# The reciprocal root of 128x64 mean squares: GpSimd pow in place of a bit estimate with Newton steps on VectorE

## The chip, the cores and the metric

The kernel runs on one core of one Trainium2 chip. The metric is the time of one execution on the device, in microseconds (us). The time before is the median of three runs. Beside it stands one profiled execution, whose trace is read below. Engines are named as in the profile: PE is TensorE's matmul, PEld its weight load, DVE VectorE, ACT ScalarE, POOL GpSimd, SP SyncE.

## The reference

One decoder layer works on x of 16 sequences, 128 tokens and 256 features, in float32. It has three parts, each added to its input and followed by a layer norm: an attention without softmax, a causal convolution of products with a context, and a feed-forward part with 4-bit weights. The change is in the attention:

```python
q = (q @ fq1_w.T + fq1_b) * (q @ fq2_w.T + fq2_b)       # k likewise; 16 heads of 16
s = jnp.where(mask, einsum('bhncd,bhnmd->bhncm', qc, kc), 0.0)
o = (inter + intra).reshape(B, H, L, dk)
o = o * jax.lax.rsqrt(jnp.mean(o * o, axis=-1, keepdims=True) + EPS) * norm_w
o = o.transpose(0, 2, 1, 3).reshape(B, L, D)
return o @ wo.T
```

So each token has 16 mean squares, one for each head, and each needs the reciprocal of its root.

## The kernel before

The 16 sequences go in four groups (g = 0 to 3) of NB = 4 sequences, 512 tokens. While the attention and the convolution of group g run (the front), the feed-forward part of group g-1 runs between them on the same engines, in 16 slots; group 0 has no such partner, and the last group's feed-forward part runs alone at the end. `schedule` writes the order out by hand, and every engine runs its own list in this one order, so an engine that waits holds up all that stands behind it in its list. In a slot the parts of the feed-forward are `gate`, `up` and `down`, and after each comes a third of the slot's front stages:

```python
slots[4] = [("sums", 0), ("sums", 1), ("rms", 0)]
slots[5] = [pause, pause, ("wide", 0)]
slots[6] = [("factor", 0), pause, pause]
slots[7] = [("outproj", 0), ("outproj", 1), pause]
slots[8] = [("norm", 0), pause, ("x1T", 0)]
```

The stages around the change are these. `squares` (ACT, L522) squares the attention's output. `sums` (PE, L973) sums the squares of each head with a matmul into 128x64 values in PSUM, 64 being 4 sequences by 16 heads. `rms` (DVE, L686 to L704) makes `mean_sq` of them and from that `inv_rms`. `wide` (ACT, L528) copies each of the 64 values 16 times, to 128x1024. `factor` transposes that on PE (L984), copies it out of PSUM on ACT (L535), and multiplies the attention's output by it on DVE (L710). `outproj` is the output projection (PE, L991), `norm` the first layer norm, whose reciprocal root is two pows of 128x2 values on POOL (`rstd`, L383).

The feed-forward part of a slot is: `gate` and `up` matmuls on PE (`split_mm`, L904 to L906), the gelu on ACT (L579), `inner` on DVE (L855, which waits for `up` and the gelu), `inner_hi` on ACT (L585), `split` on DVE (L849), and the `down` matmuls of the slot before. The 4-bit weights are unpacked beside group 0 and part of group 1, a piece at a time, by `unpack` on DVE (L634, L641, L651, L655) and ACT (L483, which waits for L634). In group 0 a piece follows the stage `rms`; in group 1 a piece opens every slot.

POOL has nothing in the stages `sums`, `rms`, `wide` and `factor` in the kernel before: its last work before them is a spread of q for the scores (L389), and its next is `rstd` of the first layer norm.

Of the kernel before, what the change touches and what calls it, by code (L numbers as in the profile page):

```python
# [14 lines left out]
I32 = mybir.dt.int32  # L15
ALU = mybir.AluOpType
# [3 lines left out]
P = 128  # L20
B, S, D = 16, 128, 256
H, DK = 16, 16
NB = 4
# [12 lines left out]
NIBBLE = (1 << 31) | (7 << 22)  # L36
LN_EPS = 1e-5
RMS_EPS = 1e-5
STEPS = 10


def count(eng, sem, per_group, g, k):

    value = per_group * g + k
    if value <= 0:
        return
    eng.wait_ge(sem, value)
# [6 lines left out]
def decoder_layer(nc, x, xT, ctx, ctxT, wq, wk, wvT, woT, fT, bias, skip, toep,  # L54
# [7 lines left out]
    with ExitStack() as stack:  # L62
        def sb(name, shape, dt=F32):
            return stack.enter_context(nc.sbuf_tensor(name, shape, dt))

        def sem(name):
            return stack.enter_context(nc.semaphore(name))
# [18 lines left out]
        minus_half = sb("minus_half", [P, 1])  # L86
# [23 lines left out]
        ctx_sb = sb("ctx_sb", [P, NB, D])  # L110
        mean_sq = sb("mean_sq", [P, NB * H])
        inv_rms = sb("inv_rms", [P, NB * H])
        newton = sb("newton", [P, NB * H])
        ve = sb("ve", [P, 3, NB])
        st = sb("st", [P, 3, NB, 6])
        mv = sb("mv", [P, 3, NB, 2])
# [19 lines left out]
        def sems(*names):  # L136
            return [sem(n) for n in names]
# [19 lines left out]

        dve_const, bd_ready, qk_ready, sm_ready, on_ready, z_ready, conv_ready = sems(
            "dve_const", "bd_ready", "qk_ready", "sm_ready", "on_ready", "z_ready", "conv_ready")
        ms_ready, newton_step, rms_ready, half_ready, sk_ready, x2lo_ready, inter_ready, ilo_ready = sems(  # L160
            "ms_ready", "newton_step", "rms_ready", "half_ready", "sk_ready", "x2lo_ready", "inter_ready", "ilo_ready")
        nibble_ready, bits_ready, deq_ready, wlo_ready = sems(
            "nibble_ready", "bits_ready", "deq_ready", "wlo_ready")

# [40 lines left out]
        conv = [("conv", h) for h in range(CH)]  # L205
# [15 lines left out]
        def with_piece(name, k):  # L221

            return name in ("rms", "factor", "norm", "x1T") or name == "score" and k % 2 == 1
# [6 lines left out]
        def schedule(eng, turn, front, gate, up, down, unpack, finish):  # L230

            pieces = iter(range(NU + 2))

            def beside(times=1):
                for _ in range(times):
                    for n in pieces:  # L240
                        unpack(n)
                        break

            def run(g, stages):
                for name, k in stages:
                    if name in front:
                        front[name](g, k)

            def slot(prev, g, s, times=(0, 0, 0)):
                each = -(-len(slots[s]) // 3)  # L250
                for i, part in enumerate((gate, up, down)):
                    beside(times[i])
                    part(prev, s)
                    if g is not None:
                        run(g, slots[s][i * each:(i + 1) * each])

            beside(START)
            turn(None, None, 0, lambda pair: beside(pair % 2))
            for s in range(NT):
                for stage in slots[s]:  # L260
                    run(0, [stage])
                    if with_piece(*stage):
                        beside()
            turn(None, 0, 1, lambda pair: beside(pair // 2))
            for s in range(NT):
                slot(0, 1, s, SECOND[s])
            for g in range(2, G):
                turn(g - 2, g - 1, g)
                for s in range(NT):
                    slot(g - 1, g, s)  # L270
            turn(G - 2, G - 1, None)
            for s in range(NT):
                slot(G - 1, None, s)
            finish()
# [80 lines left out]
        def _(pool):  # L355
# [23 lines left out]
            def rstd(g, ln):  # L379

                for j in range(2):
                    count(pool, ve_ready[ln], 2, g, j + 1)
                    nc.gpsimd.tensor_tensor(ve[:, ln, 2 * j:2 * j + 2], ve[:, ln, 2 * j:2 * j + 2],  # L383
                                            minus_half[:].broadcast_to([P, 2]), ALU.pow).then_inc(rstd_ready[ln], 1)

            def spread(g, v):

                mt, b = spread_waits(pool, g, v)
                nc.gpsimd.tensor_tensor(qbd[:, v % 2, :].rearrange("p (h c) -> p h c", c=S),  # L389
                                        qT_sb[:, mt, b * S:(b + 1) * S].unsqueeze(1).broadcast_to([P, 4, S]),  # L390
                                        quad_sel[:].unsqueeze(2).broadcast_to([P, 4, S]),
                                        ALU.mult).then_inc(spread_ready[1], 1)

            def score(g, v):

                if v + 2 < 8 and v % 2:
                    spread(g, v + 2)

            def norm(g, _):
                rstd(g, 0)  # L400

# [33 lines left out]
            def turn(done, prev, g, beside=nothing):  # L435
# [6 lines left out]
                if done is not None:  # L442
# [2 lines left out]
                    count(pool, res_ready, NB, done, NB)  # L445
                    pool.dma_start(out_v[:, bass.ds(at, NB), :], res_sb).then_inc(stored, 16)

            schedule(pool, turn, {"score": score, "norm": norm, "x1T": x1T, "conv": conv}, nothing, nothing, nothing, nothing,
                     lambda: rstd(G - 1, 2))


        @block.scalar
        def _(act):
# [70 lines left out]
            def wide(g, _):  # L524

                count(act, ms_mm, 2, g, 2)
                count(act, rms_ready, 1, g, 1)
                nc.scalar.activation(rms_sb[:].rearrange("p k (n e) -> p (k n) e", e=DK),  # L528
                                     inv_rms[:].unsqueeze(2).broadcast_to([P, NB * H, DK]), ACT.Copy)\
                    .then_inc(wide_ready, 1)  # L530

            def factor(g, _):
                for mt in range(KT):
                    count(act, rT_mm, 2, g, mt + 1)
                    nc.scalar.activation(fac_sb[:, mt, :], fb[mt][:, :], ACT.Copy).then_inc(rT_ready, 1)  # L535

            def x1T(g, _):
                for j in range(KT):
                    count(act, x1T_mm, 2, g, j + 1)
                    nc.scalar.activation(x1T_sb[:, j, :], fb[2 + j][:, :], ACT.Copy).then_inc(x1T_ready, 1)  # L540
# [52 lines left out]
        def _(dve):  # L593
# [88 lines left out]
            def rms(g, _):  # L682
                count(dve, ms_mm, 2, g, 2)
                if g:
                    count(dve, wide_ready, 1, g, 0)
                nc.vector.tensor_scalar(mean_sq[:], fb[0][:, 0:NB * H], 1.0 / DK, RMS_EPS, ALU.mult, ALU.add)\  # L686
                    .then_inc(ms_ready, 1)


                count(dve, ms_ready, 1, g, 1)  # L690
                nc.vector.tensor_scalar(newton[:].bitcast(I32), mean_sq[:].bitcast(I32), 1, None,
                                        ALU.logical_shift_right).then_inc(newton_step, 1)
                count(dve, newton_step, STEPS, g, 1)
                nc.vector.tensor_scalar(inv_rms[:].bitcast(I32), newton[:].bitcast(I32), -1, 0x5f3759df,
                                        ALU.mult, ALU.add).then_inc(newton_step, 1)
                for i in range(3):
                    count(dve, newton_step, STEPS, g, 3 * i + 2)
                    nc.vector.tensor_tensor(newton[:], inv_rms[:], inv_rms[:], ALU.mult).then_inc(newton_step, 1)
                    count(dve, newton_step, STEPS, g, 3 * i + 3)
                    nc.vector.scalar_tensor_tensor(newton[:], newton[:], -0.5, mean_sq[:], ALU.mult, ALU.mult)\  # L700
                        .then_inc(newton_step, 1)
                    count(dve, newton_step, STEPS, g, 3 * i + 4)
                    nc.vector.scalar_tensor_tensor(inv_rms[:], newton[:], 1.5, inv_rms[:], ALU.add, ALU.mult)\
                        .then_inc(rms_ready if i == 2 else newton_step, 1)  # L704

            def factor(g, _):
                count(dve, o_mm, 8, g, 8)
# [149 lines left out]
            def finish():  # L857
# [19 lines left out]
                for b in range(NB):  # L877
                    dve.wait_ge(rstd_ready[2], 2 * g + b // 2 + 1)
                    nc.vector.tensor_scalar(res_sb[:, b, :], res_sb[:, b, :], mv[:, 2, b, 0:1], ve[:, 2, b:b + 1],
                                            ALU.subtract, ALU.mult).then_inc(res_ready, 1)  # L880

            schedule(dve, turn, {"score": score, "rms": rms, "factor": factor, "outproj": outproj, "norm": norm,
                                 "conv": conv}, nothing, inner, split, unpack, finish)

# [274 lines left out]
```

## Time and profile before

| what | value |
|---|---|
| median of 3 runs | 585.72 us (584.79 to 586.55) |
| the profiled execution's own time | 585.73 us |
| span of its instructions | 584.0 us |
| mean granted TensorE clock | 0.963 |
| busy: PE, DVE, ACT, POOL | 532.6, 382.8, 157.0, 133.5 us |

The span runs from the first to the last instruction; 1.7 us of the execution's own time lie around it. Busy time is the sum of an engine's instructions. An engine's idle time costs only where the engine that sets the end waits for it. The granted clock is a share of TensorE's full rate.

### The profile page before, as it was taken

What the parts mean: (1) busy time and instruction counts of PE and PEld (TensorE: products, weight loads), DVE (VectorE), ACT (ScalarE), POOL (GpSimd) and SP (SyncE); (2) the same over time, 40 slices, a digit from 0 to 9 for tenths busy, and PEclk for the clock granted to TensorE, in tenths of its full rate; (3) what the DMA queues carried; (4) which work ended last, traced back from release to release, by engine and by line L of the source; (5) the groups of instructions that cost most, each with busy time, mean ns of one, the idle gap of its engine ahead of it and who ended that gap; (6) DMA issues with size and microseconds to landing.
All of it is one profiled execution on the core that took longest, in us unless ns stands there. A gap on an engine that the chain in (4) does not pass through costs nothing.

```text
span 584.0 us, 8537 instructions
## 1 busy us (share of the span) xinstructions
PE 532.6 (91%) x3152; PEld 426.8 (73%) x3152; DVE 382.8 (66%) x814; ACT 157.0 (27%) x291; POOL 133.5 (23%) x195
## 2 busy tenths in 40 slices
PE   5974699889999899999999999999999999599994
PEld 4733477746878788755888888856888887488883
DVE  4595799877688976875454767865454667633334
ACT  3432101352343112242232111342322111132220
POOL 2020285110004453121004452120014451200001
PEclk9995789989999999999999999999999999699998
DMA  7411332221121110031001110040001110100001
GB/s 204 119 52 42 95 108 70 66 66 33 36 80 51 52 46 9 1 114 68 1 0 46 53 40 10 0 145 1 1 5 54 44 47 0 36 1 2 0 1 36
DMA packets 25258, 26.80 MB, mean 46 GB/s; under 512 B 2817, under 2 KB 22785, under 8 KB 25217
## 3 DMA queue, kind: packets, MB, share of 16 engines
q1 hardware_dynamic: 14208, 15.73, 9.2%
q10 hardware_dynamic: 10576, 8.95, 5.3%
q0 software_dynamic: 432, 1.57, 0.8%
q8 instruction: 25, 0.41, 0.3%
q14 instruction: 17, 0.13, 0.1%
HBM read 24.15 MB, written 2.10 MB: 45 GB/s over the span
## 4 chain that ended last, share of the span: by engine, by line
PE 80%; DVE 12%; issue 3%; ACT 2%; POOL 1%; DMA 1%; ACTq 0%; POOLq 0%; DVEq 0%
PE bank L904 18%; PE bank L906 17%; PE bank L905 17%; PE bank L1014 5%; PE bank L951 5%; PE bank L1015 5%; PE bank L1017 4%; PE bank L991 3%; PE bank L961 2%; DVE qbd L677 2%; DVE weight L634 1%; PE bank L973 1%; DMA wo_sb<-in_woT 1%; PE bank L1023 1%; DVE ffn_lo L641 1%
## 5 line engine op out<-in xcount | busy, mean ns | idle before, releaser
L904 PE MATMUL bank<-x2T_lo,ffn_hi 128*128 128x512 f32 x256 | 111.8, 437 | 5.2 <-DVE x2T_lo L839 4.8
L855 DVE TENSOR_TENSOR inter<-bank,inter 128x512 f32<-128x512 f32 x64 | 44.2, 690 | 100.0 <-PE bank L906 99.8
L906 PE MATMUL bank<-x2T_hi,ffn_hi 128*128 128x512 f32 x256 | 102.5, 400 | 0.0
L905 PE MATMUL bank<-x2T_hi,ffn_lo 128*128 128x512 f32 x256 | 102.4, 400 | 0.0
L433 POOL TENSOR_TENSOR qbd<-qT_sb,ctxT_sb 128x256 f32<-128x256 f32 x128 | 80.4, 650 | 81.7 <-PE bank L1017 66.6
L383 POOL TENSOR_TENSOR ve<-ve,minus_half 128x2 f32<-128x2 f32 x24 | 16.9, 723 | 278.8 <-DVE ve L727 207.9
L904 PE MATMUL bank<-ffn_lo,inter_hi 128*128 128x256 f32 x256 | 77.1, 301 | 1.2 <-DVE inter_lo L849 0.8
L585 ACT ACTIVATE inter_hi<-inter 128x512 fp32r<-128x512 f32 x64 | 40.4, 632 | 138.5 <-DVE inter L855 138.5
L906 PE MATMUL bank<-ffn_hi,inter_hi 128*128 128x256 f32 x256 | 72.0, 281 | 0.0
L905 PE MATMUL bank<-ffn_hi,inter_lo 128*128 128x256 f32 x256 | 71.9, 281 | 0.0
L579 ACT ACTIVATE inter<-bank 128x512 f32<-128x512 f32 x64 | 38.1, 595 | 116.6 <-PE bank L906 116.5
L849 DVE TENSOR_TENSOR inter_lo<-inter,inter_hi 128x512 fp32r<-128x512 f32 x64 | 50.4, 787 | 23.8 <-PE bank L906 16.1
L904 PEld LDWEIGHTS bank<-x2T_lo,ffn_hi 128*128 128x128 f32 x256 | 48.9, 191 | 19.9 <-issue 8.5
L906 PEld LDWEIGHTS bank<-x2T_hi,ffn_hi 128*128 128x128 f32 x256 | 48.9, 191 | 12.0
L905 PEld LDWEIGHTS bank<-x2T_hi,ffn_lo 128*128 128x128 f32 x256 | 49.0, 192 | 8.3
L904 PEld LDWEIGHTS bank<-ffn_lo,inter_hi 128*128 128x128 f32 x256 | 48.2, 188 | 5.0 <-ACT inter_hi L585 2.0
L905 PEld LDWEIGHTS bank<-ffn_hi,inter_lo 128*128 128x128 f32 x256 | 48.4, 189 | 1.8
L764 DVE TENSOR_TENSOR qbd<-bank,ctxT_sb 128x256 f32<-128x256 f32 x128 | 47.7, 413 | 2.4 <-PE bank L1017 2.4
L906 PEld LDWEIGHTS bank<-ffn_hi,inter_hi 128*128 128x128 f32 x256 | 48.1, 188 | 0.0
L769 DVE TENSOR_REDUCE gate_q<-qbd 128x64 f32<-128x512 f32 x64 | 43.9, 686 | 2.2
L1014 PE MATMUL bank<-qbd,toep_sb 128*128 128x256 f32 x128 | 39.9, 394 | 4.1 <-POOL qbd L433 2.6
L951 PE MATMUL bank<-qbd,kT_sb 64*128 64x512 f32 x128 | 36.2, 644 | 3.2 <-DVE qbd L677 2.7
(116 smaller groups left out, 796.5 us busy)
## 6 DMA issues: line engine op xcount, KB each, us to landing
toep_sb<-in_toep ACTq DMA_DIRECT2D x64, 128.0 KB, 2.1
xT_sb<-in_xT SPq DMA_DIRECT2D x4, 512.0 KB, 5.9
ctxT_sb<-in_ctxT SPq DMA_DIRECT2D x4, 512.0 KB, 4.8
x_sb<-in_x SPq DMA_DIRECT2D x4, 512.0 KB, 5.9
ctx_sb<-in_ctx SPq DMA_DIRECT2D x4, 512.0 KB, 6.8
out<-ctxT_sb POOLq DMA_DIRECT2D x3, 512.0 KB, 3.4
raw_w<-in_gate_p SPq DMA_DIRECT2D x8, 128.0 KB, 2.3
raw_s<-in_gate_s SPq DMA_DIRECT2D x8, 128.0 KB
```

Of the source, the lines that this page charges most:

```text
L433: nc.gpsimd.tensor_tensor(pairs(kv_sb, h % 2)[:, kt], v_i, c_j, ALU.mult).then_inc(kv_ready, 1)
L579: nc.scalar.activation(inter[:, n % 2, :], gate_ps[:, :], ACT.Gelu_apprx_tanh).then_inc(gelu_ready, 1)
L585: nc.scalar.activation(inter_hi[:, n % 2, :], inter[:, n % 2, :], ACT.Copy).then_inc(ihi_ready, 1)
L764: last = nc.vector.tensor_tensor(pairs(z_sb, h % 2)[:, lt], fb[h % 2][:, :].rearrange("p (k b j i) -> p k b j i", k=KT, b=NB, i=CI)[:, lt] ...
L769: nc.vector.tensor_reduce(conv_sb[:, :, :, h * CI:(h + 1) * CI], pairs(z_sb, h % 2), AX.X, ALU.add)\
L849: nc.vector.tensor_tensor(inter_lo[:, n % 2, :], inter[:, n % 2, :], inter_hi[:, n % 2, :].bitcast(F32), ALU.subtract).then_inc(ilo_ready, 1)
L855: nc.vector.tensor_tensor(inter[:, n % 2, :], up_ps[:, :], inter[:, n % 2, :], ALU.mult).then_inc(inter_ready, 1)
L904: nc.tensor.matmul(ps, w_hi, x_lo, start=start, stop=False, skip_group_check=True)
L905: nc.tensor.matmul(ps, w_lo, x_hi, start=False, stop=False, skip_group_check=True)
L906: return nc.tensor.matmul(ps, w_hi, x_hi, start=False, stop=stop, skip_group_check=True)
L951: last = nc.tensor.matmul(score_ps(g, v)[r][:, :], kT_sb[rows, mt, b * S:(b + 1) * S], qbd[rows, v % 2, :], start=True, stop=True)
L1014: nc.tensor.matmul(fb[h % 2][:, 0:n], diag, kv[:, 0:n], start=True, stop=True)
```

## The change

The stage `rms` of DVE keeps its first instruction, which makes `mean_sq`. Its eleven others are taken out: a shift, a multiply-add on the bits, and three rounds of three Newton instructions, each of which waits for the one before. In their place POOL gets a stage `rms` with one instruction, a tensor_tensor with pow of the 128x64 `mean_sq` and a constant -0.5 that is broadcast over the 64 columns. `wide` on ACT waits for it as it did for the last Newton instruction. The tile `newton` and its semaphore are gone.

```diff
-        newton = sb("newton", [P, NB * H])
...
+            def rms(g, _):
+
+                count(pool, ms_ready, 1, g, 1)
+                nc.gpsimd.tensor_tensor(inv_rms[:], mean_sq[:], minus_half[:].broadcast_to([P, NB * H]), ALU.pow)\
+                    .then_inc(rms_ready, 1)
+
...
-            schedule(pool, turn, {"score": score, "norm": norm, "x1T": x1T, "conv": conv}, nothing, nothing, nothing, nothing,
+            schedule(pool, turn, {"score": score, "rms": rms, "norm": norm, "x1T": x1T, "conv": conv}, nothing, nothing, nothing, nothing,
...
                 nc.vector.tensor_scalar(mean_sq[:], fb[0][:, 0:NB * H], 1.0 / DK, RMS_EPS, ALU.mult, ALU.add)\
                     .then_inc(ms_ready, 1)
-
-
-                count(dve, ms_ready, 1, g, 1)
-                nc.vector.tensor_scalar(newton[:].bitcast(I32), mean_sq[:].bitcast(I32), 1, None,
-                                        ALU.logical_shift_right).then_inc(newton_step, 1)
-                count(dve, newton_step, STEPS, g, 1)
-                nc.vector.tensor_scalar(inv_rms[:].bitcast(I32), newton[:].bitcast(I32), -1, 0x5f3759df,
-                                        ALU.mult, ALU.add).then_inc(newton_step, 1)
-                for i in range(3):
-                    count(dve, newton_step, STEPS, g, 3 * i + 2)
-                    nc.vector.tensor_tensor(newton[:], inv_rms[:], inv_rms[:], ALU.mult).then_inc(newton_step, 1)
-                    count(dve, newton_step, STEPS, g, 3 * i + 3)
-                    nc.vector.scalar_tensor_tensor(newton[:], newton[:], -0.5, mean_sq[:], ALU.mult, ALU.mult)\
-                        .then_inc(newton_step, 1)
-                    count(dve, newton_step, STEPS, g, 3 * i + 4)
-                    nc.vector.scalar_tensor_tensor(inv_rms[:], newton[:], 1.5, inv_rms[:], ALU.add, ALU.mult)\
-                        .then_inc(rms_ready if i == 2 else newton_step, 1)
```

## Rows read from the trace of the kernel before

**Rows 1.** The page: busy time, share and instructions of the engines; the granted clock by slice.
```profile
PE 532.6 (91%) x3152; PEld 426.8 (73%) x3152; DVE 382.8 (66%) x814; ACT 157.0 (27%) x291; POOL 133.5 (23%) x195
...
PEclk9995789989999999999999999999999999699998
```

**Rows 2.** The page: the chain of work that ended last, by engine.
```profile
PE 80%; DVE 12%; issue 3%; ACT 2%; POOL 1%; DMA 1%; ACTq 0%; POOLq 0%; DVEq 0%
```

**Rows 3.** Timeline, group 0: start us, us, engine, line, operation [idle before it <- releaser].
```profile
49.89 0.22 DVE L686 TENSOR_SCALAR mean_sq<-bank 128x64 f32<-128x64 f32 x1 [3.42 <-PE bank L973]
...
52.68 0.23 DVE L703 SCALAR_TENSOR_TENSOR inv_rms<-newton,inv_rms 128x64 f32<-128x64 f32 x1
52.83 0.68 DVE L634 SCALAR_TENSOR_TENSOR weight<-weight,raw_s 128x512 f32<-128x512 f32 x1
...
53.54 0.63 ACT L483 ACTIVATE ffn_hi<-weight 128x512 fp32r<-128x512 f32 x1 [6.91 <-DVE weight L634]
...
54.08 1.04 ACT L528 ACTIVATE qT_sb<-inv_rms 128x1024 f32<-128x1024 f32 x1
...
55.17 1.97 PE L984 MATMUL bank<-ident,qT_sb 128*128 128x128 f32 x8 [5.32 <-ACT qT_sb L528]
```

**Rows 4.** Timelines of DVE, ACT and PE, group 1.
```profile
156.14 0.22 DVE L686 TENSOR_SCALAR mean_sq<-bank 128x64 f32<-128x64 f32 x1
...
161.14 0.68 DVE L855 TENSOR_TENSOR inter<-bank,inter 128x512 f32<-128x512 f32 x1
...
159.79 0.63 ACT L483 ACTIVATE ffn_hi<-weight 128x512 fp32r<-128x512 f32 x1 [4.29 <-DVE weight L634]
...
162.40 1.04 ACT L528 ACTIVATE qT_sb<-inv_rms 128x1024 f32<-128x1024 f32 x1
...
161.05 0.47 PE L904 MATMUL bank<-x2T_lo,ffn_hi 128*128 128x512 f32 x1 [0.42 <-ACT inter L579]
...
163.49 1.09 PE L984 MATMUL bank<-ident,qT_sb 128*128 128x128 f32 x8 [0.81 <-ACT qT_sb L528]
```

**Rows 5.** Timelines of DVE, ACT and PE, group 2.
```profile
288.88 0.22 DVE L686 TENSOR_SCALAR mean_sq<-bank 128x64 f32<-128x64 f32 x1
...
291.99 0.69 DVE L855 TENSOR_TENSOR inter<-bank,inter 128x512 f32<-128x512 f32 x1
...
292.71 0.63 ACT L585 ACTIVATE inter_hi<-inter 128x512 fp32r<-128x512 f32 x1 [1.53 <-DVE inter L855]
293.25 1.04 ACT L528 ACTIVATE qT_sb<-inv_rms 128x1024 f32<-128x1024 f32 x1
...
291.56 0.39 PE L906 MATMUL bank<-x2T_hi,ffn_hi 128*128 128x512 f32 x1
...
294.60 1.03 PE L984 MATMUL bank<-ident,qT_sb 128*128 128x128 f32 x8
```

**Rows 6.** POOL's instructions by line and shape: busy us, mean ns | idle before them.
```profile
L433 POOL TENSOR_TENSOR qbd<-qT_sb,ctxT_sb 128x256 f32<-128x256 f32 x128 | 80.4, 650 | 81.7 <-PE bank L1017 66.6 <-ACT qT_sb L540 14.7
...
L383 POOL TENSOR_TENSOR ve<-ve,minus_half 128x2 f32<-128x2 f32 x24 | 16.9, 723 | 278.8 <-DVE ve L727 207.9 <-DVE ve L875 71.0
L410 POOL TENSOR_TENSOR kT_sb<-x_sb,ctx_sb 128x512 f32<-128x512 f32 x8 | 13.0, 1622 | 0.0
...
L361 POOL MEMSET minus_half<- 128x1 f32 x1 | 0.1, 88 | 0.0
```

**Rows 7.** DVE's same two-instruction group in group 1, without and beside POOL's products.
```profile
177.68 0.49 DVE L651 TENSOR_SCALAR weight<-raw_w 128x256 int32<-128x256 int32 x2
...
183.47 1.34 DVE L651 TENSOR_SCALAR weight<-raw_w 128x256 int32<-128x256 int32 x2
```

**Rows 8.** PE after its long wait in the last group, and that stretch by windows: busy us (x), PEclk.
```profile
501.42 1.95 PE L1038 MATMUL bank<-ident,x_sb 128*128 128x128 f32 x8 [6.37 <-DVE x_sb L737]
505.20 0.77 PE L904 MATMUL bank<-x2T_lo,ffn_hi 128*128 128x512 f32 x1 [1.83 <-DVE x2T_lo L839]
...
510.03 0.48 PE L906 MATMUL bank<-x2T_hi,ffn_hi 128*128 128x512 f32 x1
...
505.00:510.00 5.00, 4.80 (x11) 3.81 (x12) 1.94 (x6) 0.60 (x1) 1.34 (x2) 0.50 0.28 97
```

More of the change, by code:

```diff
@@ L38 @@
 RMS_EPS = 1e-5
-STEPS = 10
 def count(eng, sem, per_group, g, k):
@@ L159, in decoder_layer @@
             "dve_const", "bd_ready", "qk_ready", "sm_ready", "on_ready", "z_ready", "conv_ready")
-        ms_ready, newton_step, rms_ready, half_ready, sk_ready, x2lo_ready, inter_ready, ilo_ready = sems(
-            "ms_ready", "newton_step", "rms_ready", "half_ready", "sk_ready", "x2lo_ready", "inter_ready", "ilo_ready")
+        ms_ready, rms_ready, half_ready, sk_ready, x2lo_ready, inter_ready, ilo_ready = sems(
+            "ms_ready", "rms_ready", "half_ready", "sk_ready", "x2lo_ready", "inter_ready", "ilo_ready")
         nibble_ready, bits_ready, deq_ready, wlo_ready = sems(
```

## The prediction

> **What bounds the kernel.** I read the busy shares first, then the chain of waits, then the timeline around `rms` in each group. PE is busy for 91% of the span and DVE for 66% [rows 1]; the chain that ended last runs over PE for 80% and over DVE for 12% [rows 2]. So DVE time as such is not what is scarce. The question is where PE waits for the reciprocal root, and that differs by group.
>
> In group 0 there is no feed-forward work between the stages. PE stands idle for 5.32 us until `wide` is done [rows 3]: the chain goes through `mean_sq` at 49.89, Newton until 52.91, the weight piece L634, ACT's L483 and `wide` at 54.08.
>
> In group 1 PE has feed-forward matmuls to do and waits only 0.42 us for a late gelu and 0.81 us for `wide` [rows 4]. Both come from DVE: Newton pushes the weight piece back, ACT's L483 stands 4.29 us idle for it, and gelu and `wide` are behind L483 in ACT's list.
>
> In group 2 PE never waits. The matmuls in front of the transposes follow each other without a gap, and the transposes start at 294.60 just as their turn comes [rows 5]. `wide` ends at 294.29, so it has 0.3 us to spare. Newton does not delay `inner` either: `inner` starts at 291.99, and the last `up` matmul, which it needs, ends at 291.95. Group 3 is the same picture 129.1 us later.
>
> **What is removed.** Eleven dependent DVE instructions in each of four groups. From the end of `mean_sq` (50.11) to the end of the last one (52.91) is 2.80 us of DVE a group [rows 3]. In groups 2 and 3 that is worth nothing by itself, since `inner` is held by PE there. In group 0 the weight piece starts 2.7 us sooner, and in group 1 too.
>
> **What is added.** One pow of 128x64 on POOL, of duration D, on an engine that is idle there. I add 0.1 us for the two hand-overs, DVE to POOL and POOL to ACT, an estimate. `wide` can then start at the end of `mean_sq` plus 0.1 plus D, and the transposes 1.09 us after `wide` starts (54.08 to 55.17) [rows 3]. Before and after, `wide` must be done at PE's turn:
>
> - Group 0: `wide` at 50.11 + 0.1 + D = 50.2 + D against 54.08. Change: D - 3.9. The gain ends where ACT's own L483 ends: L634 could start near 50.2, L483 would end 1.3 us after that, so `wide` starts no sooner than 51.5, a gain of at most 2.6.
> - Group 1: transposes at 156.36 + 0.1 + D + 1.09 = 157.6 + D against 163.49. Change: D - 5.9, and at best -1.2, the two waits of 0.42 and 0.81 [rows 4].
> - Groups 2 and 3: transposes at 289.10 + 0.1 + D + 1.09 = 290.3 + D against 294.60 [rows 5]. Change: D - 4.3 each, and never below 0.
>
> So the sum is 4D - 18.4 once D is over 4.7. Behind `wide` on ACT stand the next gelu and the two copies of `factor`; behind the transposes on PE stand `up` and `down` of the slot. PE is the engine that is full, so a stall there is not made up later.
>
> **How long is D?** No row has a pow of this size. The nearest is the pow of 128x2, 0.69 us at its shortest in the trace and 0.72 us on average over 24 [rows 6]. Of that little is the cost of issuing an instruction: a fill of 128x1 took 0.088 us. About 0.6 us is pow's own. The lower bound is that all of this is a fixed cost and a further column costs what a product's column does, 650 ns / 256 = 2.5 ns [rows 6]: D = 0.69 + 62 x 0.0025 = 0.85 us. The upper bound is that all but the 0.09 us goes by columns, 0.30 us each: D = 0.09 + 64 x 0.30 = 19.3 us. (Without even the fixed 0.09 it is 32 x 0.69 = 22.1 us.)
>
> The two ends are far apart, and the break-even lies near 4.3 us, low between them. What decides is that the row is a pow, not a product: two columns of pow cost as much as a product of 256, so a long sequence of operations is run for a column, and I see no reason why it should be nearly free for the next one. But a start-up cost in it is plausible as well. I take half of the 0.69 us as fixed and half by columns: D = 0.345 + 64 x 0.1725 = 11.4 us, an estimate.
>
> With D = 11.4: group 0 +7.5, group 1 +5.5, groups 2 and 3 +7.1 each, 27.2 in all.
>
> **The clock.** Stalls of that length also cost afterwards. After an idle time of 6.37 us PE came back at half clock, 1.2 in place of 2.4 GHz: from 505.20 to 510.03 twelve 512-column matmuls started 0.44 us apart, where they start 0.23 apart at full clock (eleven steps: 4.83 against 2.57) [rows 8]. So a stall of 6 to 7 us costs 2.3 us more. In groups 1 to 3 PE would stand 6.7, 7.1 and 7.1 us, and it runs at full clock there before: 3 x 2.3 = 6.8. In group 0 the clock is down already (the fourth digit of the slices is 5) [rows 1], so nothing is added. Without this the sum is 27.
>
> **Costed at nothing.** The POOL list: between the last spread and `rstd` POOL is idle (its 11 waits for `rstd` are 207.9 us) [rows 6], so nothing is late behind the pow. Contention with DVE: POOL's products stretched the same two DVE instructions from 0.49 to 1.34 us [rows 7]. The pow would lie beside a weight piece in groups 0 and 1. If that piece of some 2.3 us doubled, `inner` in group 1 would still be no later than before, because the piece starts 2.7 us sooner; in groups 2 and 3 only `inner` and `split` lie beside the pow, and they have slack on PE's side. Worth 0 to 1 us in all, taken as 0.
>
> **Sum.** 27.2 + 6.8 = 34.0 us on the profiled execution's 585.73, which is the median of the runs too (585.72): 619.7, say 620.
>
> The page GPSIMD Engine Reference of the Trainium skill (section 3.1) says that a two-input elementwise instruction on GpSimd costs about 2.6 cycles a column and is about half as fast as on VectorE. That agrees with the products here (650 ns for 256 columns), and applied to pow it would give the low end, D = 0.83 us, and the second rival's time. Its advice that elementwise work belongs on VectorE speaks against the change. The pow of 128x2 at 0.69 us already shows that this rate does not hold for pow's first columns.
>
> **The rivals.**
>
> 1. Forecast: pow goes mostly by columns, D over 5.0, PE stalls in all four groups. Chance 0.62. Its time runs from 587.5 (D = 5.0) over 620 to 651 (D = 19.3: 58.8 + 6.8) and 662 at the very end.
>
> 2. Pow is mostly fixed cost, D under 3.3. Then `wide` is in time everywhere, group 0 gains and group 1 loses its two short waits. At D = 0.85: -2.6 - 1.2 = -3.8, so 582. At D = 3: -0.9 - 1.2 = -2.1, 583.6. For it: the break in cost between 1 column of fill and 2 of pow could be a set-up; POOL's loop over many columns could overlap what two columns can't. Against it: 0.6 us is a long set-up. It is the other side, decided at D = 3.3 (-0.6 - 1.2 = -1.8 us, 0.3%). Chance 0.26.
>
> 3. D between 3.3 and 5.0: the slot between `rms` and `wide` hides the pow, group 1's gain offsets what group 0 and the little lateness in 2 and 3 cost. 584 to 587.5; at D = 4: +0.1 - 1.2 = -1.1. For it: the cover is there, it is only 4.3 us long. Chance 0.12.
>
> **How the numbers follow.** 0.3% of 585.7 is 1.8 us, about what a measurement of this kernel can tell from no change. The cases are split by just that: faster 0.26, same 0.12, slower 0.62. The likeliest case's own range is 588 to 655. The other two hold 0.38, so the range must reach down to the low bound, 582; upward it goes to the by-column bound with its clock cost, 651, and a little over: 655.
>
> **What would show it.** In the changed profile: the four pows of 128x64 and their duration, which settles the case at once; PE's idle time before L984 released by ACT's `wide`, and ACT's idle time before L528 released by POOL (absent before in all groups); in groups 2 and 3 an idle PE of D - 4.3; the granted clock just after it at half. In group 1 the gelu wait of 0.42 us gone. The prediction is wrong if pow's columns are cheap (no PE wait before L984 in groups 1 to 3), or if the stalls are shorter and the clock stays up.

## The result and the profile after

The changed kernel takes 615.25 us (median of 4 runs, 613.74 to 617.49) against 585.49 us before: a ratio of 1.0517, 95% interval 1.0495 to 1.0539, 29.8 us slower. The forecast was 620. The profiled execution took 613.74 us with a span of 612.0, 28.0 more than the span before. It is the quickest of the four, while the profiled execution before lay at the median, so the profiles show 28.0 of the 29.8 us.

The page of the changed kernel, parts 1, 2, 4 and 5:

```profile
PE 536.8 (88%) x3152; PEld 430.2 (70%) x3152; DVE 374.0 (61%) x770; ACT 157.9 (26%) x291; POOL 176.5 (29%) x199
...
PEclk9995789989979999999979999999979999689998
...
PE 74%; DVE 10%; POOL 8%; issue 2%; ACT 2%; DMA 1%; ACTq 0%; POOLq 0%; DVEq 0%
...
L400 POOL TENSOR_TENSOR inv_rms<-mean_sq,minus_half 128x64 f32<-128x64 f32 x4 | 42.9, 10730 | 65.6 <-DVE mean_sq L690 65.6
```

DVE has 44 instructions and 8.8 us less to do, and POOL 43 us more [rows 1]. POOL's share of the chain rose from 1% to 8% [rows 2], and nearly all of that share is the pow, the last line above (7% by itself). One pow of 128x64 takes 10.7 us on average, where eleven DVE instructions took 2.8. The clock's digits show three new dips to 7, one in each of groups 1 to 3.

The timelines of POOL, ACT and PE of the changed kernel in group 2, to be read beside [rows 5]. Columns: start, duration, engine, line, operation, and in brackets the idle time before it and its releaser.

```profile
300.50 10.55 POOL L400 TENSOR_TENSOR inv_rms<-mean_sq,minus_half 128x64 f32<-128x64 f32 x1 [18.45 <-DVE mean_sq L690]
...
304.04 0.63 ACT L589 ACTIVATE inter_hi<-inter 128x512 fp32r<-128x512 f32 x1 [1.53 <-DVE inter L842]
311.14 1.06 ACT L532 ACTIVATE qT_sb<-inv_rms 128x1024 f32<-128x1024 f32 x1 [6.47 <-POOL inv_rms L400]
312.11 0.58 ACT L583 ACTIVATE inter<-bank 128x512 f32<-128x512 f32 x1
...
312.25 1.97 PE L971 MATMUL bank<-ident,qT_sb 128*128 128x128 f32 x8 [6.15 <-ACT qT_sb L532]
...
314.44 0.63 PE L892 MATMUL bank<-x2T_hi,ffn_lo 128*128 128x512 f32 x1
314.87 0.63 PE L893 MATMUL bank<-x2T_hi,ffn_hi 128*128 128x512 f32 x1
...
316.15 0.63 PE L893 MATMUL bank<-x2T_hi,ffn_hi 128*128 128x512 f32 x1
316.58 0.34 PE L891 MATMUL bank<-ffn_lo,inter_hi 128*128 128x256 f32 x1
```

ACT finishes `inner_hi` at 304.67, 4.46 us after the start of `mean_sq` as before, and then stands 6.47 us for the pow. Its next gelu is behind `wide` in its list. PE, which did not wait here before, stands 6.15 us, and comes back at half clock: matmuls of 512 columns start 0.43 us apart until 316.6, and the granted clock from 312 to 316 us is 0.50.

In group 0 PE's wait before the transposes is 12.47 us, in place of 5.32 [rows 3]; in group 1 it is 6.50, in place of 0.81 [rows 4]:

```profile
61.04 1.97 PE L971 MATMUL bank<-ident,qT_sb 128*128 128x128 f32 x8 [12.47 <-ACT qT_sb L532]
...
173.23 1.97 PE L971 MATMUL bank<-ident,qT_sb 128*128 128x128 f32 x8 [6.50 <-ACT qT_sb L532]
```

From such rows the 28.0 us can be laid out. "Stage" is the time from the start of `mean_sq` to the start of the transposes.

| group | stage before | stage after | more | pow | from there to the next mean_sq (or the end), more |
|---|---|---|---|---|---|
| 0 | 5.28 | 12.43 | 7.15 | 10.92 | -1.2 |
| 1 | 7.35 | 12.40 | 5.05 | 10.90 | +1.6 |
| 2 | 5.72 | 12.04 | 6.32 | 10.55 | +2.1 |
| 3 | 5.73 | 12.05 | 6.32 | 10.55 | +1.9 |

The stages bring 24.8 us. The stretches behind the three new stalls bring 5.6, which is the clock: PE ran at half clock for 3.5, 4.3 and 3.5 us from the start of the transposes on, and each such stretch costs half its length. Ahead of and behind group 0's stage the changed profile was 2.5 us quicker (`mean_sq` starts at 48.61 in place of 49.89, which is 1.3, and the stretch behind the stage is 1.2 shorter). 24.8 + 5.6 - 2.5 gives the 28.0 but for rounding. The start is no effect of the change: in the experiments' profiles `mean_sq` of group 0 starts anywhere from 48.7 to 49.8. The stretch behind the stage is 100.97 us before and 99.79 after. In the first experiment below, whose pows are awaited just so, it is 100.9, so the 1.2 us did not come again; their cause stays open.

### The profile page after: what moved, and what is told of

The parts are those of the page before. It is cut to its first block, busy times and chain, and to the rows that moved or that the text cites. A ratio compares the mean times of both kernels' runs of the same rounds, so it can differ in the third digit from the quotient of the medians.

```text
span 612.0 us, 8497 instructions
## 1 busy us (share of the span) xinstructions
PE 536.8 (88%) x3152; PEld 430.2 (70%) x3152; DVE 374.0 (61%) x770; ACT 157.9 (26%) x291; POOL 176.5 (29%) x199
## 4 chain that ended last, share of the span: by engine, by line
PE 74%; DVE 10%; POOL 8%; issue 2%; ACT 2%; DMA 1%; ACTq 0%; POOLq 0%; DVEq 0%
PE bank L891 17%; PE bank L893 16%; PE bank L892 16%; POOL inv_rms L400 7%; PE bank L1001 5%; PE bank L938 4%; PE bank L1002 4%; PE bank L1004 4%; PE bank L978 3%; PE bank L948 2%; DVE qbd L681 1%; PE bank L971 1%; DVE weight L638 1%; PE bank L1010 1%; DMA wo_sb<-in_woT 1%
## 5 line engine op out<-in xcount | busy, mean ns | idle before, releaser
L891 PE MATMUL bank<-x2T_lo,ffn_hi 128*128 128x512 f32 x256 | 113.5, 443 | 4.8 <-DVE x2T_lo L826 4.8
L400 POOL TENSOR_TENSOR inv_rms<-mean_sq,minus_half 128x64 f32<-128x64 f32 x4 | 42.9, 10730 | 65.6 <-DVE mean_sq L690 65.6
```

The source lines that it names most:

```text
L400: nc.gpsimd.tensor_tensor(inv_rms[:], mean_sq[:], minus_half[:].broadcast_to([P, NB * H]), ALU.pow)\
L891: nc.tensor.matmul(ps, w_hi, x_lo, start=start, stop=False, skip_group_check=True)
```

## The experiments

A change in us is the difference of the medians. Ratios are to the kernel before in the same session (medians 585.12 in the first four experiments, 586.06 in the others), with 95% intervals.

### The same pow in pieces of other sizes

```diff
-                nc.gpsimd.tensor_tensor(inv_rms[:], mean_sq[:], minus_half[:].broadcast_to([P, NB * H]), ALU.pow)\
-                    .then_inc(rms_ready, 1)
+                size = 32 >> g
+                for at in range(0, NB * H, size):
+                    last = nc.gpsimd.tensor_tensor(inv_rms[:, at:at + size], mean_sq[:, at:at + size],
+                                                   minus_half[:].broadcast_to([P, size]), ALU.pow)
+                    last.then_inc(rms_ready, 1)
...
```

> The 64 columns are done by pows of 32 (group 0), 16 (group 1), 8 (group 2) and 4 columns (group 3), all of them awaited by wide. My theory (a fixed part and a part by columns, worked out from 0.69 us for 2 columns and 10.55 for 64: 0.37 + 0.159 a column): 5.5, 2.9, 1.6 and 1.0 us for one piece, 10.9, 11.7, 13.1 and 16.1 us a group, and the whole some 9 us over the changed kernel, 623. Rival, all by columns: every group takes the 10.6 us of one pow, and the time stays at 615. Rival, a loop over blocks of columns: pieces of 4 or 8 cost as much as one of 16.

One run, 624.57 us, 9.3 over the changed kernel where I expected 9; one run has no interval, so the argument rests on the durations in its trace. POOL's groups of this kernel by shape (busy us, mean ns | idle before):

```profile
L402 POOL TENSOR_TENSOR inv_rms<-mean_sq,minus_half 128x4 f32<-128x4 f32 x16 | 15.7, 999 | 18.4 <-DVE mean_sq L693 18.4
...
L402 POOL TENSOR_TENSOR inv_rms<-mean_sq,minus_half 128x8 f32<-128x8 f32 x8 | 12.9, 1629 | 18.5 <-DVE mean_sq L693 18.5
L402 POOL TENSOR_TENSOR inv_rms<-mean_sq,minus_half 128x16 f32<-128x16 f32 x4 | 11.9, 3000 | 18.4 <-DVE mean_sq L693 18.4
```

The pieces of 32 in group 0 took 11.2 us for two, so the four groups took 11.2, 11.9, 12.9 and 15.7 us, near the 10.9, 11.7, 13.1 and 16.1 expected. In the third experiment, below, 32 columns by themselves take 5.43. So the sizes 2, 4, 8, 16, 32 and 64 take 0.69, 1.00, 1.63, 3.00, 5.43 and 10.55 us (group 2's). That is a straight line of 0.37 us plus 0.16 us a column, within 0.1 us at every size. Both rivals fall: the small pieces are not free of a fixed part, and there is no block of columns that costs the same however full. Per column pow costs some 60 times a product's 2.5 ns [rows 6]. The fixed part is about half of the 128x2 row, as the prediction had taken it. The GPSIMD Engine Reference of the Trainium skill (section 3.1) gives about 2.6 cycles a column for two-input elementwise instructions. Pow does not go by that price here: a column of it costs some 60 times a product's.

### A product in the place of the pow

The reciprocal root is left out here; the instruction, its place and its waits are the same.

```diff
-                nc.gpsimd.tensor_tensor(inv_rms[:], mean_sq[:], minus_half[:].broadcast_to([P, NB * H]), ALU.pow)\
+                nc.gpsimd.tensor_tensor(inv_rms[:], mean_sq[:], minus_half[:].broadcast_to([P, NB * H]), ALU.mult)\
...
```

> The same instruction in the same place with a product in place of pow, so the reciprocal root is left out and the output is another. My theory (pow's duration alone costs, the place and the hand-overs nothing): the instruction takes 0.2 to 0.3 us, group 0 gains 2.6 and group 1 gains 1.2 us over the kernel before, 581.7, a ratio of 0.9935. Rival (the hand-over to POOL and back costs as such): not below 585.

578.56 us, ratio 0.9881 (0.9854 to 0.9907). The product took 0.29 us in groups 2 and 3 and 0.67 in groups 0 and 1, where I had expected 0.2 to 0.3; the fourth experiment comes back to this. The groups of `wide` and of the transposes in this kernel, by line and shape (busy us, mean ns | idle before them, releaser):

```profile
L532 ACT ACTIVATE qT_sb<-inv_rms 128x1024 f32<-128x1024 f32 x4 | 4.2, 1041 | 0.0
...
L971 PE MATMUL bank<-ident,qT_sb 128*128 128x128 f32 x32 | 5.1, 311 | 2.5 <-ACT qT_sb L532 2.5
```

ACT never waits for the value, and PE waits 2.5 us in all, in group 0 alone. So the place and the hand-overs cost nothing, and the rival falls. The gain is larger than I expected, 6.6 us in place of 3.8. The stages explain 4.4: group 0's went from 5.28 to 2.49, group 1's from 7.35 to 5.73 (1.6 where I had 1.2), groups 2 and 3 stayed at 5.72. In the profiles another 0.8 is in the last group's feed-forward: after the same 6.36 us wait the half clock lasted for 8 matmuls of 512 columns in place of 12. That is no effect of the product: behind this same wait, which is there in every kernel, the profiles of the first and fifth experiments have 8 as well, and others up to 15. In the profiles the rest is nearly all ahead of group 0's `mean_sq` (48.68 in place of 49.89), a start that moves by as much between kernels which are the same up to there. So 1.4 us of the median's 6.6 have no cause shown.

### POOL and DVE side by side, half of the columns each

On POOL, against the changed kernel:

```diff
-                nc.gpsimd.tensor_tensor(inv_rms[:], mean_sq[:], minus_half[:].broadcast_to([P, NB * H]), ALU.pow)\
+                nc.gpsimd.tensor_tensor(inv_rms[:, 0:32], mean_sq[:, 0:32], minus_half[:].broadcast_to([P, 32]), ALU.pow)\
...
```

and on DVE the eleven instructions of before on columns 32 to 63.

> POOL's pow on columns 0 to 31 and DVE's bit estimate and Newton steps on columns 32 to 63, side by side. My theory: pow takes 5.5 us; group 0 is 1.6 us late, group 1 not at all (Newton's own delay is as long), groups 2 and 3 1.2 us late each, the clock stays up because the waits are short: +4.0 us, 589.5, a ratio of 1.007. Rival (the cost goes with the pow's share of the work, with no cover): half of the changed kernel's 29.8 us, 600.

589.22 us, ratio 1.0058 (1.0037 to 1.0079), +4.1 us. Timelines of POOL, ACT and PE in group 2 of this kernel:

```profile
289.62 5.44 POOL L401 TENSOR_TENSOR inv_rms<-mean_sq,minus_half 128x32 f32<-128x32 f32 x1 [18.45 <-DVE mean_sq L691]
...
295.16 1.06 ACT L533 ACTIVATE qT_sb<-inv_rms 128x1024 f32<-128x1024 f32 x1 [1.36 <-POOL inv_rms L401]
...
296.27 1.09 PE L989 MATMUL bank<-ident,qT_sb 128*128 128x128 f32 x8 [1.05 <-ACT qT_sb L533]
...
297.44 0.41 PE L910 MATMUL bank<-x2T_hi,ffn_lo 128*128 128x512 f32 x1
297.68 0.39 PE L911 MATMUL bank<-x2T_hi,ffn_hi 128*128 128x512 f32 x1
```

Half the pow costs a seventh of the whole one's 29.8 us. PE waits 1.05 us in groups 2 and 3, and 0.78 in group 1 as before; in group 0 it waits 6.98 in place of 5.32. 1.7 + 0 + 1.05 + 1.05 = 3.8 us. After so short a wait the matmuls are at full rate (0.24 apart). This is the cover, seen directly: of a pow of 5.44 us, all but 1.05 is free in groups 2 and 3, that is about 4.4 us.

### The pow as well, with nobody waiting for it

This is the kernel before, Newton included, with a stage more on POOL:

```diff
+            def rms(g, _):
+                count(pool, ms_ready, 1, g, 1)
+                nc.gpsimd.tensor_tensor(unused[:], mean_sq[:], minus_half[:].broadcast_to([P, NB * H]), ALU.pow)\
+                    .then_inc(unused_ready, 1)
...
```

> The kernel before with the pow of 128x64 run as well, into a tile that nothing reads: Newton gives the value. My theory: nobody waits for the pow and it does not slow DVE, so the time is that of before, 585.5 within 0.3%. Rival (the pow holds the memory port that it shares with DVE, or is late for the next POOL work): DVE's instructions beside it are stretched as they are beside POOL's products, and several of the 29.8 us come back.

585.24 us, ratio 1.0004 (0.9989 to 1.0019). 10.6 us of POOL four times over, beside DVE's Newton, weight pieces and `inner`, cost nothing that can be measured. So POOL's own list has no part in the 29.8 us, and a pow that is under way does not slow what lies beside it enough to matter; the cost is the wait for the result.

One thing differs in the changed kernel. Here Newton stands between `mean_sq` and the weight piece; there the piece follows at once, and the pow begins while DVE is in the piece's first instruction. Timelines of the changed kernel's DVE and POOL, group 0:

```profile
48.75 0.68 DVE L638 SCALAR_TENSOR_TENSOR weight<-weight,raw_s 128x512 f32<-128x512 f32 x1
49.35 0.78 DVE L645 TENSOR_TENSOR ffn_lo<-weight,ffn_hi 128x512 fp32r<-128x512 f32 x1
50.05 0.48 DVE L655 TENSOR_SCALAR weight<-raw_w 128x256 int32<-128x256 int32 x2
...
48.91 10.92 POOL L400 TENSOR_TENSOR inv_rms<-mean_sq,minus_half 128x64 f32<-128x64 f32 x1 [10.25 <-DVE mean_sq L690]
```

That pow and group 1's took 10.92 and 10.90 us, against 10.55 in groups 2 and 3, where no piece lies beside it, and against 10.54 to 10.56 in all four groups of this experiment, where the pieces come only after Newton. The product in the pow's place shows the same step, 0.67 against 0.29. So beginning beside L638 costs a POOL instruction 0.35 to 0.38 us, whatever its length, and 0.7 us of the 24.8 are contention of this kind. The other way round little is lost: L645 took 0.78 us in place of 0.68, and the pair that POOL's products had stretched from 0.49 to 1.34 [rows 7] took 0.48 beside the pow.

### The use of the result one slot later

```diff
-        slots[5] = [pause, pause, ("wide", 0)]
-        slots[6] = [("factor", 0), pause, pause]
-        slots[7] = [("outproj", 0), ("outproj", 1), pause]
-        slots[8] = [("norm", 0), pause, ("x1T", 0)]
-        slots[9] = [pause, pause, conv[0]]
+        slots[5] = [pause, pause, pause]
+        slots[6] = [pause, pause, ("wide", 0)]
+        slots[7] = [("factor", 0), pause, pause]
+        slots[8] = [("outproj", 0), ("outproj", 1), pause]
+        slots[9] = [("norm", 0), pause, ("x1T", 0)]
+        slots[10] = [pause, pause, conv[0]]
```

with the 15 other conv stages three to a slot in slots 11 to 15, on the changed kernel.

> The changed kernel with wide and all that follows it one slot later (the 16 conv stages close up), so that in groups 1 to 3 a slot of feed-forward matmuls more lies between the pow and its turn. My theory (only what sticks out of the cover costs): group 0 has no such cover and stays 7 us late; in groups 2 and 3 PE waits about 2 us in place of 6.2, in group 1 about 1.5 in place of 6.5; waits so short leave the clock up: +12 us over the kernel before, 597. Rival (the cost belongs to the pow itself, wherever its result is used): 615 as in the changed kernel.

598.09 us, ratio 1.022 (1.0184 to 1.0255), +12.0 us. Timeline of PE in groups 1, 2 and 3 of this kernel:

```profile
175.69 1.34 PE L971 MATMUL bank<-ident,qT_sb 128*128 128x128 f32 x8 [2.29 <-ACT qT_sb L532]
...
177.25 0.63 PE L892 MATMUL bank<-x2T_hi,ffn_lo 128*128 128x512 f32 x1
177.68 0.63 PE L893 MATMUL bank<-x2T_hi,ffn_hi 128*128 128x512 f32 x1
...
308.41 1.09 PE L971 MATMUL bank<-ident,qT_sb 128*128 128x128 f32 x8 [1.94 <-ACT qT_sb L532]
...
309.61 0.63 PE L892 MATMUL bank<-x2T_hi,ffn_lo 128*128 128x512 f32 x1
310.04 0.63 PE L893 MATMUL bank<-x2T_hi,ffn_hi 128*128 128x512 f32 x1
...
440.87 1.09 PE L971 MATMUL bank<-ident,qT_sb 128*128 128x128 f32 x8 [1.93 <-ACT qT_sb L532]
...
442.03 0.40 PE L892 MATMUL bank<-x2T_hi,ffn_lo 128*128 128x512 f32 x1
442.27 0.40 PE L893 MATMUL bank<-x2T_hi,ffn_hi 128*128 128x512 f32 x1
```

With the same four pows (PE's wait in group 0 is again 12.47 us), 17 to 18 of the 29.8 us are gone. The waits in groups 1 to 3 shrank by one slot's matmuls, 4.2 us each or 12.6 in all. The cost is not the pow's but the part of it that sticks out.

Two things of my expectation failed. PE's wait in group 1 is 2.29 us and not 1.5. And the clock did fall in groups 1 and 2 (matmuls 0.43 us apart), after waits of 2.29 and 1.94 us, and stayed up in group 3 after 1.93. It fell only 0.7 and 1.1 us after PE had resumed, and stayed at half for 3.4 us each time, which costs 1.7 each, 3.4 in all. That the total came out as expected is therefore partly luck. The waits, 12.1 us more than before, and these 3.4 would make 15.5 more in the span, and the profile has 11.8; the missing 3.7 are 1.0 ahead of group 0's `mean_sq` and 2.7 in other stretches. The order of the conv stages was changed too, and the kernel before was not run with this order, so what the order gives by itself stays open.

### Two Newton rounds

```diff
-                for i in range(3):
+                for i in range(2):
```

> The kernel before with two Newton rounds in place of three: three of DVE's instructions less, 0.78 us a group. My theory (the root's duration counts in full in group 0, in group 1 until its two short waits of 1.2 us are gone, and not at all in groups 2 and 3): -0.8 - 0.8 = -1.6 us, 583.6, a ratio of 0.9973. Rival (it counts in every group): -3.1, 582.0. Rival (it counts nowhere): 585.1.

584.83 us, ratio 0.998 (0.9965 to 0.9994), -1.2 us. PE's wait in group 0 is 4.54 in place of 5.32, that is 0.78 less. In group 1 it is 0.67 in place of 0.81, and the stage went from 7.35 to 6.57, again 0.78. Groups 2 and 3 stay at 5.73. The first expectation holds; "in every group" (0.9947) and "nowhere" lie outside the interval.

### A quarter of the columns on POOL

The edit is that of the third experiment with 16 in place of 32.

> POOL's pow on 16 of the 64 columns, Newton on the other 48. By the sizes measured, the pow takes 3.0 us, less than the cover of about 4 us in every group, and about what Newton takes beside it. My theory: the time of before, 585.1 within 0.3%. Rival (a pow of any size on this path costs by its hand-overs): above 587.

585.50 us, ratio 0.9997 (0.9975 to 1.002). The pow of 16 columns takes 2.92 us and is wholly hidden, beside Newton on the other 48 columns; the hand-overs cost nothing that can be measured.

### Two rounds and another order

In group 0 a weight piece now follows the stage `wide` and no longer `rms`; in group 1 the piece of slot 5 stands behind `inner`, before the slot's last third, and no longer at the slot's beginning.

```diff
-            return name in ("rms", "factor", "norm", "x1T") or name == "score" and k % 2 == 1
+            return name in ("wide", "factor", "norm", "x1T") or name == "score" and k % 2 == 1
-        SECOND = [(1, 0, 0)] * 14 + [(0, 0, 0)] * 2
+        SECOND = [(1, 0, 0)] * 5 + [(0, 0, 1)] + [(1, 0, 0)] * 8 + [(0, 0, 0)] * 2
```

on top of the two Newton rounds.

> The kernel before with two Newton rounds and another place for one weight piece: behind wide on ACT in group 0, and behind inner on DVE in group 1, so that neither ACT's copy nor the gelu waits for a piece that DVE starts only after Newton. My theory: group 0 gains 0.8 for the round and 1.1 more since wide starts right after Newton; group 1 gains its two waits of 1.2 us: -3.1 us, 582.0, a ratio of 0.9947. Rival (the piece is then late and holds up the copy of factor or the weights): 583.6 or more.

582.26 us, ratio 0.993 (0.9906 to 0.9954), -3.8 us: the fastest kernel with the whole computation here. Timelines of its ACT in group 0 and its PE in group 1:

```profile
52.13 1.06 ACT L528 ACTIVATE qT_sb<-inv_rms 128x1024 f32<-128x1024 f32 x1 [5.58 <-DVE inv_rms L703]
53.09 0.61 ACT L483 ACTIVATE ffn_hi<-weight 128x512 fp32r<-128x512 f32 x1
...
158.98 1.09 PE L984 MATMUL bank<-ident,qT_sb 128*128 128x128 f32 x8 [0.18 <-ACT qT_sb L528]
```

`wide` now starts 0.09 us after the last Newton instruction (it ends at 52.04), and the weight's copy comes after it. Group 0's stage is 3.44 us long in place of 5.28, group 1's 6.08 in place of 7.35: 1.84 + 1.27 = 3.1, as expected. Newton's third round is 0.78 of each, so the order alone brings 1.06 in group 0 and 0.49 in group 1.

## Why the prediction was right, by its steps

**DVE's time is not what is scarce.** Right. DVE lost 8.8 us of work and the kernel became slower. In groups 2 and 3 a shorter Newton is worth nothing (with two rounds their stages took 5.73 us, as before), and in groups 0 and 1 it counts in full.

**D.** I took 11.4 us from half of the 128x2 row as fixed; it is 10.55, and 10.9 where the pow begins beside a weight piece. The step was the least certain one of all, between 0.85 and 19.3, and the sizes show why the halving was right: 0.37 fixed and 0.32 for two columns. That it came so near was partly luck, since no row told the two apart.

**The cover.** The formulas D - 3.9, D - 5.9, D - 4.3, D - 4.3 give 7.0, 5.0, 6.25 and 6.25 with the pows measured, 24.5 in all, against 24.8 in the trace. They gave 4D - 18.4 = 27.2 with my D. The hand-overs were 0.16 us together in group 2 (300.43 to 300.50, 311.05 to 311.14), where I took 0.1.

**The clock.** 5.6 us against 6.8 forecast. The mechanism was right; the size was taken from a row where PE was idle again soon after it came back, while here it was full, and full rate returned after 3.5 to 4.3 us and not 8.6. That the idle time made the difference is an argument, not shown, and the row is one draw of several: behind that same wait of 6.37 us, full rate came back after anything from 7.2 to 10.1 us in the ten profiles. The experiments with shorter waits show this term by itself: no fall after 1.05 us, a fall in two of three groups after 1.9 to 2.3, and half clock each time after 6 us or more.

**Costed at nothing.** Right in size: the pow run for nobody gave a ratio of 1.0004. The 0.7 us that there is lies inside the range of 0 to 1 us, but on the side that I had not looked at: the weight piece holds up the pow, and not the pow the piece.

**The sum.** I had 34.0 us and the medians give 29.8. The stalls were 2.4 us smaller than the 27.2 forecast and the clock 1.2 smaller than its 6.8; the rest is the 2.5 us that the changed profile was quicker elsewhere, less the 1.8 by which the medians differ more than the profiles.

**The signs.** All came: ACT's waits for POOL before `wide`, PE's waits before the transposes, 6.15 and 6.16 us in groups 2 and 3 (D - 4.3 is 6.25), half clock behind them, and in group 1 no more wait of 0.42 us for the gelu.

**The rivals.** The small-D rival would have given a gain, and the product in the pow's place shows that its mechanism is real: the stages give -4.4 us where I had computed -3.8, and the whole kernel -6.6, of which part has no cause shown. Only pow's price rules it out. The third rival's region, a pow of 3.3 to 5.0 us, was not run; the two kernels with partial pows, which keep Newton for the other columns, lie just outside it, 2.92 us with a ratio of 0.9997 and 5.43 us with 1.0058.

## What to carry to other kernels

Ask first how long the result may take before the engine that sets the end has its turn: here 4 us, with one instruction of 10.7 us in place of eleven short ones that took 2.8. Counting instructions, or moving work to an idle engine, says nothing about that. One row of an operation at one size gives no price for another size: here the two bounds from it were 0.85 and 19.3 us, and that the middle was right no row could tell; the experiment of sizes takes one run. Where a value is due soon, also look at what stands before its use in the other engine's list: in group 0, moving one weight copy behind `wide` took 1.06 us off the stage and a Newton round 0.78.

## What the runs showed of the hardware

GpSimd's pow on float32 costs 0.37 us and 0.16 us for each column of 128 values, in a straight line from 2 to 64 columns. While it runs it hardly disturbs VectorE (0.78 for 0.68 us in one instruction beside it, nothing in the total). A pow that began while VectorE was in a 128x512 scalar_tensor_tensor took 10.9 us in place of 10.55, and a product of the same size 0.67 in place of 0.29.

TensorE's granted clock fell to 1.2 GHz after a wait as short as 1.94 us in a stretch where it is otherwise full, 1.1 us after TensorE had resumed; it did not after one of 1.93 us of the same kernel, nor after any of 1.05. What tells the first two apart stays open. After one and the same wait of 6.37 us ahead of the same work, the half clock lasted from 7.2 to 10.1 us in the ten profiles, counted from TensorE's first instruction behind the wait.
